# Two of the four quarters of the q·k products of a windowed attention on GpSimd, the second queued behind the low halves of the attention weights

## The reference

```python
q = Wq·LN(x) + bq;  k = Wk·ctx + bk;  v = Wv·ctx + bv     # over the 64 channels, for each batch entry
k, v = pad(k, 8 left, 7 right), pad(v, 8 left, 7 right)    # along the 512 positions
dots[b,h,t,w] = sum_d q[b,h,d,t] * k[b,h,d,t+w] * 8**-0.5  # 8 heads of 8 channels, 16 windows
attn = softmax(dots, over w)
out[b,h,d,t] = sum_w attn[b,h,t,w] * v[b,h,d,t+w]
x = x + tanh(g) * (Wo·out + bo)
```

## Time and profile before

| | |
|---|---|
| median of 3 runs | 1103.3 us (1102.65 to 1105.46) |
| profiled execution | 1103.59 us |
| its span, first to last instruction | 1101.8 us |
| mean granted TensorE clock | 0.968 of full speed |
| windowed attention | about the first 240 us of the span |
| busy share of the span | TensorE 92%, VectorE 64%, GpSimd 50%, ScalarE 39% |

### The profile page before, as it was taken

How to read it: one execution, slowest core, us unless ns; L and a number is a source line. 1 busy time by engine, 2 the same in 40 slices (tenths; PEclk the granted TensorE clock), 3 DMA queues, 4 the chain that set the end, 5 groups by cost and what they waited for, 6 DMA issues and landing times. The chain is left out here.

```text
span 1101.8 us, 13713 instructions
## 1 busy us (share of the span) xinstructions
PE 1016.5 (92%) x4712; PEld 735.0 (67%) x4712; DVE 702.1 (64%) x1100; ACT 427.3 (39%) x1226; POOL 545.9 (50%) x389
## 2 busy tenths in 40 slices
PE   5688887879778999999999999999999969999998
PEld 1344443446566777777777777777777747888787
DVE  4899998875756677777777777765565544222223
ACT  3233333223112655455545554554534523312121
POOL 3566666454726767657766678663441002223021
PEclk9899999888988999999999999999999999999999
DMA  8000000011021533333433444331100006120001
GB/s 274 1 1 1 0 1 1 1 33 58 20 73 54 162 115 106 116 106 125 132 94 122 131 159 139 133 110 30 33 35 1 1 1 198 39 58 15 1 1 76
DMA packets 60964, 75.93 MB, mean 69 GB/s; under 512 B 8444, under 2 KB 44068, under 8 KB 60888
## 3 DMA queue, kind: packets, MB, share of 16 engines
q1 hardware_dynamic: 56032, 57.66, 16.4%
q0 software_dynamic: 4144, 17.04, 5.0%
q10 hardware_dynamic: 720, 0.36, 0.1%
HBM read 64.37 MB, written 10.68 MB: 68 GB/s over the span
## 5 line engine op out<-in xcount | busy, mean ns | idle before, releaser
L1377 POOL TENSOR_TENSOR shared<-shared 128x512 f32<-128x512 f32 x64 | 83.6, 1306 | 146.9 <-DVE shared L1528 146.2
L1449 ACT ACTIVATE c_xn<-c_xn,c_mn 128x64 f32<-128x64 f32 x256 | 86.4, 340 | 107.6 <-DVE c_mn L1542 107.6
L763 PE MATMUL ps<-woh,oh 128*128 128x512 f32 x256 | 103.7, 405 | 4.7 <-DVE ol L1554 4.7
L763 PE MATMUL ps<-xh,wqh 128*128 128x512 f32 x256 | 107.2, 419 | 0.0
L375 POOL TENSOR_TENSOR r<-r 128x1024 f32<-128x1024 f32 x32 | 76.0, 2374 | 56.5 <-DVE r L548 56.5
L1526 DVE TENSOR_TENSOR shared<-ps,cs 128x512 f32<-128x512 f32 x80 | 55.1, 689 | 74.7 <-PE ps L765 70.6
L765 PE MATMUL ps<-woh,ol 128*128 128x512 f32 x256 | 101.4, 396 | 0.0
L764 PE MATMUL ps<-wol,oh 128*128 128x512 f32 x256 | 101.1, 395 | 0.0
L765 PE MATMUL ps<-xh,wql 128*128 128x512 f32 x256 | 101.0, 394 | 0.0
L764 PE MATMUL ps<-xl,wqh 128*128 128x512 f32 x256 | 100.3, 392 | 0.0
L548 DVE TENSOR_TENSOR r<-ps,vpad 128x512 f32<-128x512 f32 x128 | 80.6, 686 | 17.9 <-PE ps L638 17.3
(11 more groups left out here) (179 smaller groups left out, 2413.6 us busy)
## 6 DMA issues: line engine op xcount, KB each, us to landing
stage<-in_wq SPq DMA_DIRECT2D x16, 512.0 KB
stage<-in_wo SPq DMA_DIRECT2D x16, 512.0 KB
w_wide<-dq SPq DMA_DIRECT2D x32, 172.0 KB, 2.4
wf<-w_wide SPq DMA_DIRECT2D x20, 256.0 KB, 3.0
qraw<-in_gate_qweight SPq DMA_DIRECT2D x16, 172.0 KB
qraw<-in_up_qweight SPq DMA_DIRECT2D x16, 172.0 KB
qraw<-in_down_qweight SPq DMA_DIRECT2D x10, 256.0 KB
w_down<-dq SPq DMA_DIRECT2D x10, 256.0 KB, 2.7
```

The source lines that it names most:

```text
L763: pe.matmul(dst, lh, rh, start=(first and c == 0), stop=False)
L1377: pool.tensor_tensor(qT[:, h * TPH:(h + 1) * TPH, :, p - 1, :], turn(ra), turn(rb), ALU.add)\
L1449: act.activation(part, part, ACT.Exp, scale=-1.0, bias=mn[:, c % 2, u:u + 1], accum_out=sm[:, c % 2, u:u + 1]).then_inc(exp_ready, 1)
```

## The change

VectorE gives quarter 2 to GpSimd. GpSimd now makes quarter 2 where it made quarter 3 (first thing in a step), and quarter 3 after the two low halves and `scale_of_rows`, ahead of the four sums of `r`. The counts of the waits follow: two quarters a tile are counted on `prod_ready` (VectorE) and two on `last_prod_ready` (GpSimd).

```diff
-        PARTS = WIN // GW
-        PART_LAST = PARTS - 1
+        VECTOR_PARTS, POOL_PARTS = 2, 2
...
-                    products(pool, q[:, :], s, PART_LAST).then_inc(last_prod_ready, 1)
+                    products(pool, q[:, :], s, VECTOR_PARTS).then_inc(last_prod_ready, 1)
                 if s >= 1:
                     low_half(i, 0)
                     low_half(i, 1)
                 if s + 2 < NT:
                     scale_of_rows(s + 2)
+                if s < NT:
+                    products(pool, q[:, :], s, VECTOR_PARTS + 1).then_inc(last_prod_ready, 1)
...
 # ScalarE, before it writes kpad and q
-                    act.wait_ge(prod_ready, PART_LAST * (i - 1))
-                    act.wait_ge(last_prod_ready, i - 1)
+                    act.wait_ge(prod_ready, VECTOR_PARTS * (i - 1))
+                    act.wait_ge(last_prod_ready, POOL_PARTS * (i - 1))
...
-                    act.wait_ge(last_prod_ready, i)
+                    act.wait_ge(last_prod_ready, POOL_PARTS * i)
...
 # VectorE
-                if s < NT:
-                    part_of_products(s, 2)
                 if s + 2 < NT:
                     normalise(s + 2)
...
 # TensorE, queries and reduce_heads
-                    pe.wait_ge(prod_ready, PART_LAST * i)
+                    pe.wait_ge(prod_ready, VECTOR_PARTS * i)
...
-                        pe.wait_ge(prod_ready, PART_LAST * i + 2)
+                        pe.wait_ge(prod_ready, VECTOR_PARTS * i + 2)
                     else:
-                        pe.wait_ge(prod_ready, PART_LAST * (i + 1))
-                        pe.wait_ge(last_prod_ready, i + 1)
+                        pe.wait_ge(prod_ready, VECTOR_PARTS * (i + 1))
+                        pe.wait_ge(last_prod_ready, POOL_PARTS * (i + 1))
```

## The result

The changed kernel takes 1114.14 us in the median of 4 runs (1112.49 to 1114.47); the kernel before 1103.99 in the median of 4 runs (1102.65 to 1105.46). The ratio is 1.0088, with a 95% interval of 1.0073 to 1.0104: slower by 10.15 us, where 10.5 us and a time of 1114 were forecast. The profiled execution is the fastest of the four: it took 1112.49 us with a span of 1110.5, that is 8.7 us above the span before.

The account below looks back on a forecast made before the run. It took the chain through low half, turning back, spreads and products to bound a step, not VectorE. Blocked `normalise` and step 0 add 1.5 + 0.34 + 2 × 2.74 + 2 × 1.58 = 10.5 us: 1114, range 1110 to 1121.

Parts of the forecast that it names:

- What bounds a step: Attention steps: the chain low half, turning back, spread, product, spread binds; VectorE's relief gains 0.23 us a full-clock step.
- Who comes first at the ports: After `scale_of_rows`: GpSimd issues 0.06 us ahead, so `normalise` waits for its whole 4.18 us quarter on the shared SBUF ports.
- rival 1: VectorE gets the SBUF ports first, `normalise` takes its 0.54 us: +1.0 us, 1104.6, no change; chance 0.09.
- The size in steps 1 to 5: Attention steps with `normalise` blocked: +0.34 us in step 1, +2.74 in 2 and 4, +1.58 in 3 and 5.
- Step 0: First, serial attention step: GpSimd's second quarter ends at 23.5, TensorE's upper-half sums began at 22.03; +1.5 us.
- Steps 6 and 7: Last attention steps, without `normalise`: the quarter lies in GpSimd's idle hole; 0, with −2.2 us at full clock in the range.
- Rival 2: TensorE's clock falls a second time, behind its wait for spread 3, in steps 1 to 5: 5.5 us more, 1119.6; chance 0.14.

Follow-up runs that it names:

- experiment 4: The kernel before with quarter 2 left out on VectorE from step 1 on and made by nobody; 1102.57 us, ratio 0.9995.
- experiment 1: The changed kernel, but GpSimd waits for the normalised rows before its second quarter (steps 0 to 5); 1107.01 us, ratio 1.0031 to the kernel before.
- Experiment 7: The kernel before, but ScalarE takes the two high halves of the weights ahead of the copies of k and v; 1098.75 us, ratio 0.9963.
- Experiment 2: The kernel before, all three quarters still on VectorE, plus a spare GpSimd quarter behind `scale_of_rows` that nobody reads; 1112.75 us, ratio 1.0086.
- experiment 8: The changed kernel with step 0 as before, GpSimd's second quarter behind the normalised rows, and ScalarE's high halves first; 1093.85 us, ratio 0.9910 to the kernel before.
- experiment 3: The changed kernel with only two of the second quarter's four windows on GpSimd, the others on VectorE ahead of `normalise`; 1103.36 us, ratio 1.0006 to the kernel before.
- experiment 5: The changed kernel with step 0 as before (VectorE makes quarter 2, GpSimd one quarter only); 1113.84 us, ratio 1.0090 to the kernel before.
- experiment 6: The changed kernel with step 0 as before and GpSimd's second quarter behind the normalised rows; 1102.77 us, ratio 0.9992 to the kernel before.

## Why the prediction was right

**What bounds a step** held. VectorE's relief alone brings 0.26 us in a full-clock step (experiment 4) and 0.24 with the port free (experiment 1); the forecast worked out 0.23. Experiment 7 bears it out from the other side: with the low halves 1.0 us earlier a full-clock step stays at 25.4 us, so there VectorE was the later of the two by a little; in the steps whose clock had fallen the chain was.

**Who comes first at the ports** held. It was argued from 0.06 us and the ties of the earlier trace rows; in all six steps with a `normalise` in the loop GpSimd started 0.06 to 0.07 us ahead and `normalise` lasted 4.37 to 4.40 us; rival 1 didn't come. Experiments 1 and 2 show the cause from both sides: the order alone takes the loss away in the loop, the load alone brings it. No run here changed the form of `normalise`, so which property of it lets GpSimd's quarter keep it out isn't shown.

**The size in steps 1 to 5** held to 0.1 us: 9.0 us against 9.05 measured. The quarter beside a waiting VectorE took 4.16 to 4.18 us, as the forecast needed.

**Step 0 was undersized.** "+1.5" counted the late sums only. They did begin 1.54 us later behind the first product (23.06 − 12.22 against 22.03 − 12.73). But the term put the clock behind the sums at nothing. The timeline of the changed kernel, then two stretches of it from 20.9 on:

```profile
23.06 2.86 PE L586 MATMUL ps<-prod,sel 128*32 128x512 f32 x16 [2.29 <-POOL prod L309]
25.84 1.84 PE L571 MATMUL ps<-xn,w 128*128 128x512 f32 x2
```

```profile
20.90:24.30 3.40, 1.24 (x12) 0.60 (x16) 2.34 (x1) 0.54 (x1) 2.06 (x1) 0.94 0.95 268
24.30:27.70 3.40, 3.40 (x12) 0.91 (x5) 0.00 (x0) 0.60 (x1) 0.00 (x0) 0.56 0.04 5
```

Behind the wait of 2.29 us the clock was at its lower level for most of the next stretch (0.56), and the same sums took 2.86 us in place of 1.92. The step lost 3.2, 1.65 of it beyond the late sums. Whether the longer wait is the cause of that part stays open. In experiment 8, whose step 0 has the old order, the same sums took 3.64 us behind a wait of 0.79 us, and the step came to 22.91 us (as in experiment 4):

```profile
13.20:36.11 22.91, 11.27 (x49) 3.33 (x47) 16.37 (x14) 6.61 (x12) 8.88 (x3) 0.78 0.51 172
```

So the low clock falls on these sums without the longer wait, too.

**Steps 6 and 7 were put at 0, and that term failed.** They took 24.14 and 23.00 us against 25.50 and 25.71 in the trace before, at a clock of 1.00 against 0.93 and 0.87. Experiment 2 has 24.15 and 23.01 with all of VectorE's quarters in place, so it isn't the relief. For step 6 it doesn't look like the chance of one execution either: it takes 24.12 to 24.15 us at a clock of 1.00 in the four traces with a stretched `normalise` (the changed kernel, experiments 2, 3 and 5), and 25.50 to 25.53 at 0.93 in the four with a free one and the old order of ScalarE (the kernel before, experiments 1, 4 and 6). Step 6 of experiments 5 and 6:

```profile
174.70:198.82 24.12, 20.20 (x92) 9.74 (x92) 19.39 (x25) 7.32 (x11) 20.28 (x8) 1.00 0.00 1
...
164.22:189.75 25.53, 21.78 (x92) 10.37 (x92) 19.48 (x25) 7.33 (x11) 20.28 (x8) 0.93 0.00 1
```

Step 7 is less regular: 23.0 us in three of the first four and 25.34 in experiment 5; 25.7 or 24.2 to 24.3 in the others. So some of the loss comes back once `normalise` ends. Why the clock stays up there no run isolates. The range had 2.2 us for it; it was 4.1.

**The total was partly luck.** Outside steps 1 to 5 the trace has −0.5 at the start, 1.7 more than forecast in step 0, −4.1 in steps 6 and 7 and +1.0 behind them. That is −1.9 together, so that the span rose by 8.7 us and not by 10.5. The median of the four runs lies 1.65 us above the profiled one, and so the forecast time was met more closely than its terms.

**Rival 2 was mis-sized and rare.** The forecast's argument against it held in 12 of 15 blocked steps (the changed kernel, experiments 2 and 5): the clock had fallen earlier in the step, TensorE's wait ahead of spread 3 was only 0.2 to 1.6 us, and no second fall followed. Three steps came to that wait at full clock and waited 2.70 us. One of these shows the second fall, at 2.3 us and not 1.1: the low stretch there lies on the sums and spreads of the window loop, which follow one another on TensorE.

## What to carry to other kernels

Before work goes to GpSimd, list the VectorE instructions that will run beside it, and pick out those that the trace shows stretched when GpSimd is busy: here one such instruction of half a microsecond, released by the instruction ahead of the new work, waited for all of it. If the work must go there, put it behind that instruction with a wait; 0.6 us of delay on the idle engine took away a block of 3.8 us on the busy one (4.39 to 0.55). And an engine that is 94% busy in a step may have little to give: leave some of its work out once and see. Here 2.28 us less brought 0.26 us, and 1.2 to 1.3 us a step only when the chain beside it was shortened as well.

## What the runs showed of the hardware

A stretched VectorE instruction counts as busy from its start: 4.39 us in the profile for 0.54 us of work, and none of the 3.85 us that it was held up counts as idle. The 0.98 us in its bracket are the wait for `scale_of_rows`, ahead of its start.

A fall of TensorE's clock costs by where it lies: 1.1 us on a step of the kernel before (in step 5 the turning back took 1.80 us, first row below, in place of the 1.09 of step 4); nothing in a step where another wait ended later (28.11 us at 0.94 and at 1.00); and 2.3 us in the window loop (30.42 against 28.11). With the high halves first TensorE's wait for the low half was 1.66 us in place of 2.65 (second row, of experiment 8), and in both experiments steps 2 to 5 all ran at 1.00:

```profile
140.67 1.80 PE L622 MATMUL ps<-ident,stack 128*128 128x128 f32 x8 [2.65 <-POOL stack L350]
...
88.01 1.09 PE L626 MATMUL ps<-ident,stack 128*128 128x128 f32 x8 [1.66 <-POOL stack L349]
```
